# Decoder layer on one core: the opening written out by engine, and the output bias moved from TensorE to VectorE

## Chip, cores and metric

One core of one Trainium2 chip. The time is device microseconds of one execution; the number compared is the median of the timed runs.

## What is computed

For 16 sequences of 256 tokens and width 128 (x), and a context of 1601 rows of width 96 for each:

```python
x = x + attention(layernorm(x))             # one head of 128, with biases
x = x + cross(layernorm(x), context)        # 16 heads of 64, bias bo at the output
x = x + ffn(x)                              # router picks 31 tokens; small attention and MLP on them
# cross: q = x@Wq; k, v = context@Wk, context@Wv
#        sim = q k^T / 8; softmax over the 1601 rows; out@Wo + bo
```

All in float32 as far as the result goes. The cross attention is nearly all of the work: 16 sequences x 16 heads x 256 queries x 1601 keys.

## The kernel before, in words

The key and query weights of the cross attention are multiplied into one matrix per head (G, 96 x 128), the value and output weights into another (M). With these, scores are products of context rows and of the queries in the context's 96 columns, and the output is M applied to weighted sums of context rows. The arithmetic is float16 in two parts: a high part (AH, ChT, EH, Ch) and a low part (AL, ClT, EL, Cl).

**The stream.** A batch is 104 tiles: 8 pairs of heads, each with 13 tiles of 124 context rows. The stream runs over 16 x 104 tiles. For each tile n TensorE makes the scores ("st", L541 and L542, into PSUM banks 4 and 5), ScalarE takes exp into PF (L860), for each pair of tiles VectorE or ScalarE rounds PF to EH (L1042, L867), GpSimd takes the rest EL = PF - EH (L1512), and eight tiles later TensorE multiplies EH and EL with the context ("av", L558 and L560, into bank 6). After 13 tiles ScalarE copies the sums out (L876), GpSimd normalises them (L1520), TensorE transposes them ("turn_u", L615) and, for each four heads, multiplies with M ("proj", L605, bank 7) and VectorE adds the result to X (L1106). For the first quarter of heads the projection starts with products of a row of ones and the row xbo, the output bias bo (L603).

Beside it runs, for each batch, the preparation of the next: the shift of the softmax (an upper bound of the scores for each query) by "diff" and "base" products (L579, banks 2-3 and 0-1), a ReLU of ScalarE (L882), and "fold", a maximum of VectorE (L1065); then "placemax" transposes the maxima (L633), ScalarE scales them (L911) and a DMA of SyncE puts them into row 96 of AH (L1609). Further the layer norms, the self attention, the queries (L589, L896, L1074), the scale of the context, its split and its transposes (L626, L903), and the choice of tokens. The small steps share bank 7.

**Order.** The order is written by hand: plan(b, ...) gives each step of batch b a place, a tile number k, and whole_order(engine) lays the steps of all kinds into one list. Every engine runs through this list in the same order, save for steps that LATER moves by a few places for one engine. Engines skip steps in which they have nothing to do, and wait on semaphores for what others must have done, so a step stands behind whatever is ahead of it in its engine's list. SyncE follows TensorE's list. The steps ahead of the first tile form the opening; there, too, one list serves all engines. In it come in this order: layer norm and self attention of batch 0, the angles of the rotary embedding ("trig"), the scale of the context and of G ("sigma", "gtop"), G for the two halves of heads ("gm" q, parts 0 and 1, L708), its split ("gsplit", L958 and L1248), the context's split and transposes, the first queries, and the maximum of the first two heads. M (parts 2 and 3 of "gm", L720, copied by L1217) is made at places 0 to 3 of the stream. In the opening the small steps go round four banks, 7, 6, 0, 1.

BUSY names steps before which TensorE makes idle products of the identity (L520, results not used). keep_busy(step) issues them ahead of the step's own wait.

## Time and profile before

| | us |
|---|---|
| median of three timed runs (2243.27 to 2247.11) | 2245.14 |
| the profiled execution | 2249.61 |
| its span in the profile | 2248.4 |
| TensorE busy | 2154.0 |
| GpSimd busy | 1926.4 |
| ScalarE busy | 1831.9 |
| VectorE busy | 1781.7 |

All numbers below come from the one profiled execution, whose own time lies 1.2 us above its span and 4.5 us above the median of the timed runs. PE is TensorE, PEld its weight loads, DVE VectorE, ACT ScalarE, POOL GpSimd, SPq the DMA issues of SyncE. Matmuls overlap, and their ends are modelled: the distance between the starts of two, not their duration, says what one costs. In a group "xN" is the number of instructions; a float32 product counts two.

### The profile page before, as it was taken

How to read it: one execution, taken by the hardware profiler on the slowest of the kernel's cores; microseconds unless marked ns; L12 is line 12 of the kernel's file. 1: busy time of each engine (PE TensorE's matmuls, PEld its weight loads, DVE VectorE, ACT ScalarE, POOL GpSimd, SP SyncE). 2: the span in 40 equal slices, each digit the busy share in tenths (PEclk: the TensorE clock that was granted, in tenths of full speed). 3: DMA queues.
4: the chain of work that ended last, by engine and by line, in shares of the span. 5: the costliest groups of instructions: out<-in, count | busy, mean ns of one | idle time of the engine just before them, and what ended most of it. 6: DMA issues, size and time to landing. Idle time of an engine off the chain costs nothing.

```text
span 2248.4 us, 58064 instructions
## 1 busy us (share of the span) xinstructions
PE 2154.0 (96%) x22151; PEld 1574.0 (70%) x22151; DVE 1781.7 (79%) x3728; ACT 1831.9 (81%) x3125; POOL 1926.4 (86%) x1112
## 2 busy tenths in 40 slices
PE   7899999999999999999999999999999999999998
PEld 4677777777777767777777777767777777676665
DVE  6777888787887888878787788877868788886755
ACT  5888888888888888888788887888878888888862
POOL 2799999999998989898898898888978898898982
PEclk9999999999999999999999999999989999999999
DMA  3110000000000000000000000000000000000000
GB/s 69 37 43 13 2 9 5 2 13 2 13 2 4 11 2 13 2 13 2 11 13 2 13 2 2 13 2 13 2 11 12 2 13 2 2 1 2 2 8 13
DMA packets 17221, 22.15 MB, mean 10 GB/s; under 512 B 5601, under 2 KB 14834, under 8 KB 16946
## 3 DMA queue, kind: packets, MB, share of 16 engines
q1 hardware_dynamic: 15842, 18.24, 3.0%
q8 instruction: 178, 2.92, 0.5%
q14 instruction: 97, 0.79, 0.1%
q10 hardware_dynamic: 1104, 0.20, 0.1%
HBM read 16.20 MB, written 2.10 MB: 8 GB/s over the span
## 4 chain that ended last, share of the span: by engine, by line
PE 68%; DVE 12%; ACT 10%; issue 8%; POOL 3%; DVEq 0%; ACTq 0%; POOLq 0%
PE PS L541 12%; PE PS L579 12%; PE PS L542 11%; PE PS L558 10%; PE PS L560 9%; PE PS L605 4%; DVE EH L1042 4%; ACT PF L860 3%; DVE over L1065 3%; POOL EL L1512 2%; ACT EH L867 2%; ACT over L882 2%; PE PS L589 2%; PE PS L615 2%; DVE junk L1308 1%
## 5 line engine op out<-in xcount | busy, mean ns | idle before, releaser
L1512 POOL TENSOR_TENSOR EL<-PF,EH 124x1024 f16<-124x1024 f32 x828 | 1760.8, 2149 | 229.1 <-DVE EH L1042 111.2
L860 ACT ACTIVATE PF<-PS 124x512 f32<-124x512 f32 x1664 | 973.9, 603 | 251.5 <-PE PS L542 240.4
L558 PE MATMUL PS<-Ch,EH 123*128 123x97 f16 (+1 forms) x6656 | 769.8, 208 | 22.0 <-POOL EL L1512 11.2
L560 PE MATMUL PS<-Cl,EL 123*128 123x97 f16 (+1 forms) x6656 | 766.5, 208 | 0.0
L1042 DVE TENSOR_SCALAR_CACHE_REDUCE EH<-PF 124x1024 f16<-124x1024 f32 x621 | 745.1, 1209 | 9.2 <-ACT PF L860 9.0
L558 PEld LDWEIGHTS PS<-Ch,EH 123*128 123x128 f16 (+1 forms) x6656 | 611.4, 98 | 186.7 <-issue 61.1
L560 PEld LDWEIGHTS PS<-Cl,EL 123*128 123x128 f16 (+1 forms) x6656 | 600.8, 98 | 171.6 <-issue 4.6
L1065 DVE CUSTOM_DVE_ANT_1 over<-over,PS 128x806 f32<-128x806 f32 x512 | 506.0, 988 | 200.0 <-ACT over L882 110.8
L541 PE MATMUL PS<-AH,ChT 97*124 97x512 f16 x1664 | 649.6, 390 | 9.9 <-ACT PF L860 5.8
L542 PE MATMUL PS<-AL,ClT 96*124 96x512 f16 x1664 | 637.1, 383 | 0.0
L882 ACT ACTIVATE over<-PS 128x806 f32<-128x806 f32 x512 | 434.4, 848 | 36.1 <-PE PS L579 15.5
L541 PEld LDWEIGHTS PS<-AH,ChT 97*124 97x124 f16 x1664 | 226.7, 136 | 108.1 <-ACT PF L860 35.6
L579 PE MATMUL PS<-ChT,AH 96*128 96x403 f16 x1024 | 263.5, 338 | 13.7 <-DVE pmax L1065 13.5
L579 PE MATMUL PS<-KD,AH 96*128 96x403 f16 x1024 | 263.0, 338 | 0.8 <-ACT over L882 0.4
L542 PEld LDWEIGHTS PS<-AL,ClT 96*124 96x124 f16 x1664 | 228.3, 137 | 32.8 <-issue 0.6
L867 ACT ACTIVATE EH<-PF 124x1024 f16<-124x1024 f32 x211 | 223.7, 1061 | 0.0
L1074 DVE SCALAR_TENSOR_TENSOR AL<-PS,qscale,AH 96x512 f16<-96x512 f32 x128 | 95.5, 746 | 133.2 <-ACT AH L896 133.1
L1520 POOL TENSOR_TENSOR Un<-U,rden_u 128x384 f32<-128x384 f32 x127 | 114.6, 903 | 17.4 <-DVE rden_u L1095 17.4
L896 ACT ACTIVATE AH<-PS,qscale 96x512 f16<-96x512 f32 x128 | 87.5, 684 | 23.0 <-PE PS L589 22.9
L605 PE MATMUL PS<-M,UT 128*128 128x128 f32 x768 | 105.3, 283 | 0.1
L579 PEld LDWEIGHTS PS<-ChT,AH 96*128 96x128 f16 x1024 | 78.9, 99 | 34.7 <-DVE pmax L1065 19.2
L605 PEld LDWEIGHTS PS<-M,UT 128*128 128x128 f32 x768 | 91.9, 191 | 4.4 <-ACT UT L887 0.5
(234 smaller groups left out, 1816.2 us busy)
## 6 DMA issues: line engine op xcount, KB each, us to landing
Cf<-in_ctx SPq DMA_DIRECT2D x16, 546.0 KB
X<-in_x SPq DMA_DIRECT2D x16, 128.0 KB, 2.5
out_x<-X SPq DMA_DIRECT2D x16, 128.0 KB, 1.7
msk<-in_attention_mask SPq DMA_DIRECT2D x4, 256.0 KB, 4.3
AH<-mh SPq DMA_DIRECT2D x63, 2.0 KB
Cf<-in_ctx SPq DMA_DIRECT2D x16, 53.6 KB
xWqT<-in_xWqT SPq DMA_DIRECT2D x2, 256.0 KB, 7.5
xWo<-in_xWo SPq DMA_DIRECT2D x2, 256.0 KB, 4.2
```

The costliest lines, as they stand in the source:

```text
L541: pe.matmul(o, ChT[j][:, t, :], AH[:, cs], start=True, stop=False)
L542: pe.matmul(o, ClT[j][:, t, :], AL[:, cs], start=False, stop=True).then_inc(sg("st"), 1)
L558: pe.matmul(PS[:, 6, u0:u0 + DC + 1], EH[0:kr, r, qs], Ch[j][0:kr, t, :], start=(t == 0 and q == 0), stop=False, skip_group_check=True)
L560: m = pe.matmul(PS[:, 6, u0:u0 + DC + 1], EL[0:kr, r, qs], Cl[j][0:kr, t, :], start=False, stop=(t == KT - 1), skip_group_check=True)
L579: m = pe.matmul(PS[:, bank + n, 0:NKEY], AH[0:DC, ht * P:(ht + 1) * P], src[:, n * NKEY:(n + 1) * NKEY], start=True, stop=True)
L605: m = pe.matmul(PS[:, kb, t * D:(t + 1) * D], UT[:, t, c, :], M[:, qd * QC + c, :], start=(c == 0 and qd > 0), stop=(c == QC - 1))
L860: act.activation(PF[:, n % PRING, :], PS[0:KP, 4 + n % 2, :], ACT.Exp).then_inc(sg("ex"), 1)
L867: act.activation(EH[:, r - 1:r + 1, :], PF[:, f - 1:f + 1, :], ACT.Copy, scale=KEEP).then_inc(sg("eh_act"), 1)
L882: act.activation(over[:, i % 2, :, :], PS[:, 2:4, 0:NKEY], ACT.Relu).then_inc(sg("relu"), 1)
L1042: dve.tensor_scalar(EH[:, r - 1:r + 1, :], PF[:, f - 1:f + 1, :], KEEP, None, ALU.mult, ALU.add, accum_out=esum[:, r // 2:r // 2 + 1]).the ...
L1065: dve.tensor_tensor_reduce(out=o, in0=o, in1=PS[:, 0:2, 0:NKEY], scale=1.0, scalar=LEAST, op0=ALU.add, op1=ALU.max, accum_out=pmax[:, b % ...
L1512: pool.tensor_tensor(EL[:, r - 1:r + 1, :], PF[:, f - 1:f + 1, :], EH[:, r - 1:r + 1, :], ALU.subtract).then_inc(sg("lo_pool"), 1)
```

## The change

- The opening is written out for each engine on its own (a new function opening(engine)), instead of one list for all. The products of M move from places 0 to 3 of the stream into the opening, two of them into other banks (0 and 2 instead of 6), with waits of their own; the fifth diff and base wait for them. The split of the second half of G goes ahead of the first placing of the maxima, the fold of the first maxima ahead of the scale of the second half of G, the products of the probabilities' transposes ahead of that of G's maximum.
- Idle products: one more at sa_t and at sa_qk, one less at sa_o, none at sa_turn, ctx_t and placemax; new ones ahead of diff 1 and base 1 to 3.
- The output bias: xbo is loaded as a row for each of the 128 partitions, and a new step "bias" of VectorE adds it to X of the batch (128x256), two places after the step sa_f of that batch; for batch 0 at the end of the opening. The products of ones and xbo at the first projection of each batch go. The projection's add waits for it once.
- GpSimd no longer fills a row of ones, and fills the last row of ChT only after the angles are done (a wait on trig_in).
- SyncE loads the two bias columns b_q and b_k ahead of the weights w_q and w_k.
- All places of the stream stay as they are, but for the products of M.

```diff
--- before.py
+++ after.py
@@ -156,7 +156,6 @@
                  (SEL_PLACE - 2, ("sel_count", b - 1, 0)), (SEL_PLACE + 3, ("sel_count", b - 1, 1)),
                  (SEL_PLACE + 13, ("sel_rank", b - 1))]
     if b == 0:
-        todo += [(k, ("gm", q, part)) for k, (q, part) in enumerate(((0, 2), (0, 3), (1, 2), (1, 3)))]
         todo += [(9, ("ln_stats0", 1)), (12, ("ln0", 1))]
         todo += [(10 + 4 * x, ("load_x", x)) for x in range(2, B)] + [(72, ("load_rest",))]
         todo += [(10, ("ctx_max", 1)), (18, ("sigma", 1)), (22, ("ctx_scale", 1))]
@@ -167,12 +166,37 @@
     if n < B:
         todo += [(TILES + k, step) for k, step in ahead(n) if k < 0]
         split = AV_LAG + 17 * (b == 0)
-        todo += [(split + 0, ("ctx_hi", n, 0)), (split - 1, ("ctx_hi", n, 1))]
+        todo += [(split, ("ctx_hi", n, 0)), (split - 1, ("ctx_hi", n, 1))]
         todo += [(split + 4, ("ctx_lo", n, 0)), (split + 8, ("ctx_lo", n, 1))]
         todo += list(zip(TURN_PLACES, transposes_of(n))) + [(TURN_PLACES[1] + 1, ("keys", n))]
         q = [k + 9 * (b == 0) for k in SA_PLACES]
         todo += list(zip((*q[:6], q[5] + 5, q[5] + 10, q[6]), self_attention(n)[2:]))
+        todo += [(q[6] + 2, ("bias", n))]
     return sorted(todo + beside.get(b, []), key=lambda x: x[0])
+
+
+def opening(engine):
+
+    stats, norm, turn, qk, val, sc, probs, att, stats1, norm1, x2 = self_attention(0)
+    high, low = context_of(0)[:2], context_of(0)[2:]
+    turns = transposes_of(0)
+    folds = [maximum(0, ht) for ht in range(4)]
+    moved = [("gm", q, part) for q, part in ((0, 2), (0, 3), (1, 2), (1, 3))]
+    if engine == "pe":
+        out = [turn, qk, ("wvo",), sc, ("sigma", 0), ("gm", 0, 0), ("gm", 0, 1), val, probs, ("gtop", 0), att]
+        out += turns[:2] + [("gm", 1, 0), ("gm", 1, 1), ("load_ctx", 1), x2, ("q", 0, 0)] + folds[0] + folds[1] + [("gtop", 1)]
+        out += folds[2] + folds[3] + turns[2:3] + moved[:1]
+        return out + [("placemax", 0, 0, 2)] + moved[1:2] + turns[3:] + moved[2:3] + [("q", 0, 1)] + moved[3:]
+    if engine == "act":
+        out = [turn, ("trig",), qk, sc, probs] + high + [("gsplit", 0)] + turns[:2] + [x2, ("q", 0, 0)]
+        out += [f[0] for f in folds] + [("gsplit", 1)] + turns[2:3]
+        return out + [("placemax", 0, 0, 2)] + turns[3:] + [("q", 0, 1)]
+    if engine == "dve":
+        out = [stats, norm, ("trig",), qk, ("ctx_max", 0), ("wvo",), sc, ("sigma", 0), ("gmax", 0), ("ctx_scale", 0), val]
+        out += [("gtop", 0), att, stats1, ("gsplit", 0), norm1, ("keys", 0), x2] + low + [("q", 0, 0)]
+        out += folds[0] + [("gmax", 1)] + folds[1] + [("gtop", 1)] + folds[2] + folds[3]
+        return out + [("gsplit", 1)] + moved[:3] + [("q", 0, 1)] + moved[3:] + [("bias", 0)]
+    return [stats, ("consts",), ("more_consts",), stats1]
 
 
 def whole_order(engine):
@@ -183,16 +207,7 @@
     def put(n, kind, *a):
         stream.append((n + shift.get(kind, 0), len(stream), (kind, *a)))
 
-    first = self_attention(0)
-    turns = transposes_of(0)
-    out += [first[0], ("consts",), *first[1:3], ("trig",), first[3], ("wvo",), ("ctx_max", 0), first[5], first[4]]
-    out += [("gm", 0, 0), ("gm", 0, 1), ("gmax", 0), ("sigma", 0), ("gtop", 0)]
-    split = context_of(0)
-    out += [first[6], ("more_consts",), ("ctx_scale", 0), first[7], first[8]] + split[:2]
-    out += [("gsplit", 0), split[2]] + turns[:2] + [("gm", 1, 0), ("gm", 1, 1)]
-    out += [first[9], split[3], ("load_ctx", 1), first[10], ("keys", 0), ("gmax", 1), ("q", 0, 0)]
-    out += maximum(0, 0)[:2] + [("gtop", 1)] + maximum(0, 0)[2:] + maximum(0, 1) + maximum(0, 2) + maximum(0, 3) + turns[2:3]
-    out += [("placemax", 0, 0, 2)] + turns[3:] + [("gsplit", 1), ("q", 0, 1)]
+    out += opening(engine)
     groups, todo = beside_plan(), []
     for n in range(TOTAL + AV_LAG):
         b, k = n // TILES, n % TILES
@@ -288,8 +303,7 @@
         wkT = sb("wkT", [P, P])
         wvo = sb("wvo", [P, P])
         cols = sb("cols", [P, 3])
-        xbo = sb("xbo", [1, P])
-        ones = sb("ones", [1, P])
+        xbo = sb("xbo", [P, P])
         crow = sb("crow", [P, P])
         fwq = sb("fwq", [P, 2, P])
         fwv = sb("fwv", [P, P])
@@ -410,7 +424,7 @@
         out_dram = out.rearrange("b (p t) d -> p b t d", t=T)
         X4 = X[:, :, :].rearrange("p (b t) d -> p b t d", t=T)
         rows = [slice(32 * b4, 32 * b4 + 32) for b4 in range(4)]
-        GM_BANKS = ((2, 3, 6, 6), (4, 5, 6, 6))
+        GM_BANKS = ((2, 3, 6, 0), (4, 5, 2, 6))
         HEAD_BANKS = (7, 6, 0, 1)
         TAIL_BANKS = (0, 1, 2, 3, 4, 6, 7)
         LAST_TURN = ("turn_u", B - 1, QD - 1, 1)
@@ -420,12 +434,11 @@
 
         M_CHUNKS = [of for m in range(HP // 2)
                     for of in (((2 * m, 0),), ((2 * m, P), (2 * m + 1, -64)), ((2 * m + 1, 64),))]
-        CONST_IDENT, CONST_TURNS, CONST_ALL = 5, 13, 29
+        CONST_IDENT, CONST_TURNS, CONST_ALL = 5, 12, 28
         HALVES = (slice(0, 7), slice(7, KT))
 
-        BUSY = {("sa_t", 0): 8, ("sa_qk", 0): 1, ("sa_turn", 0): 3, ("sa_o", 0): 2,
-                ("ctx_t", 0, 0, 0, 7): 2, ("sa_f", 0): 4, ("q", 0, 0): 4, ("diff", 0, 0): 3,
-                ("placemax", 0, 0, 2): 5,
+        BUSY = {("sa_t", 0): 9, ("sa_qk", 0): 2, ("sa_o", 0): 1, ("sa_f", 0): 4, ("q", 0, 0): 4, ("diff", 0, 0): 3,
+                ("diff", 0, 1): 2, ("base", 0, 1): 2, ("base", 0, 2): 2, ("base", 0, 3): 3,
                 ("turn_u", B - 1, QD - 1, 0): 4, ("proj", B - 1, QD - 1): 1, ("sel_row", B - 1): 17,
                 ("last_gather", NG - 1): 5, ("c_turn", NG - 1): 8, ("c_qkm", NG - 1): 3, ("c_tqk", NG - 1): 5,
                 ("c_sc", NG - 1): 4, ("c_texp", NG - 1): 12, ("c_att", NG - 1): 2, ("c_tatt", NG - 1): 1,
@@ -433,7 +446,7 @@
                 ("c_scat", NG - 1, 0): 2}
 
 
-        BUSY_LATER = (("sa_f", 0), ("q", 0, 0), ("diff", 0, 0), ("placemax", 0, 0, 2))
+        BUSY_LATER = (("sa_f", 0), ("q", 0, 0), *((k, 0, ht) for k in ("diff", "base") for ht in range(4)))
 
 
         order = whole_order("pe")
@@ -574,6 +587,8 @@
                         w.wait_ge(sg("relu"), i - 1)
                     else:
                         w.wait_ge(sg("fold"), i - 1)
+                    if i == 5:
+                        w.wait_ge(sg("m_done"), 3 if k == "diff" else 2)
                     src = KD[j][:, :] if k == "diff" else ChT[j][0:DC, :, :].rearrange("p t k -> p (t k)")
                     for n in range(2):
                         m = pe.matmul(PS[:, bank + n, 0:NKEY], AH[0:DC, ht * P:(ht + 1) * P],
@@ -598,12 +613,9 @@
                     for t in range(T):
                         if t == T - 1:
                             w.wait_ge(sg("ut_last" if last else "ut"), 1 if last else T * i)
-                        if qd == 0:
-                            w.wait_ge(sg("in_xbo"), 16)
-                            pe.matmul(PS[:, kb, t * D:(t + 1) * D], ones[0:1, :], xbo[0:1, :], start=True, stop=False)
                         for c in range(QC):
                             m = pe.matmul(PS[:, kb, t * D:(t + 1) * D], UT[:, t, c, :], M[:, qd * QC + c, :],
-                                          start=(c == 0 and qd > 0), stop=(c == QC - 1))
+                                          start=(c == 0), stop=(c == QC - 1))
                     m.then_inc(sg("pj_mm"), 1)
                 elif k == "turn_u":
                     b, qd, t = s.a
@@ -712,8 +724,12 @@
                         w.wait_ge(sg("in_xm"), 96)
                         if (q, part) == (0, 2):
                             w.wait_ge(*last_of_head(6))
+                        elif (q, part) == (0, 3):
+                            w.wait_ge(sg("fold"), 4)
+                        elif (q, part) == (1, 2):
+                            w.wait_ge(sg("relu"), 4)
                         else:
-                            w.wait_ge(sg("m_done"), 2 * q + part - 2)
+                            w.wait_ge(sg("m_done"), 1)
                         for c in range(QC):
                             of = M_CHUNKS[(2 * q + part - 2) * QC + c]
                             for n, (j, first) in enumerate(of):
@@ -1102,6 +1118,7 @@
                 elif k == "proj":
                     b, qd = s.a
                     w.wait_ge(sg("pj_mm"), i)
+                    w.wait_ge(sg("bo_added"), b + 1)
                     w.wait_ge(sg("pj_x"), i - 1)
                     dve.tensor_tensor(X[:, T * b:T * b + T, :], PS[:, bank_of(s), 0:T * D].rearrange("p (t d) -> p t d", d=D),
                                       X[:, T * b:T * b + T, :], ALU.add).then_inc(sg("pj_x"), 1)
@@ -1203,6 +1220,13 @@
                     dve.scalar_tensor_tensor(out=X2T[:, 1, b % 2, :], in0=X2T[:, 0, b % 2, :], scalar=-KEEP / REST,
                                              in1=PS[:, bank_of(s), 0:S], op0=ALU.mult,
                                              op1=ALU.add).then_inc(sg("x2_lo"), 1)
+                elif k == "bias":
+                    b, = s.a
+                    w.wait_ge(sg("xn2"), i)
+                    w.wait_ge(sg("in_xbo"), 16)
+                    dve.tensor_tensor(X[:, T * b:T * b + T, :], X[:, T * b:T * b + T, :],
+                                      xbo[:, :].rearrange("p (o d) -> p o d", o=1).to_broadcast([P, T, D]),
+                                      ALU.add).then_inc(sg("bo_added"), 1)
                 elif k == "wvo":
                     w.wait_ge(sg("wvo_mm"), 1)
                     w.wait_ge(sg("in_wvo"), 64)
@@ -1465,7 +1489,7 @@
             for s in orders["pool"]:
                 k, i = s.kind, s.i
                 if k == "consts":
-                    const(pool.memset(ones[:, :], 1.0), pool.memset(lower[:, :, :, :], 1.0), pool.memset(headmask[:, :], 1.0),
+                    const(pool.memset(lower[:, :, :, :], 1.0), pool.memset(headmask[:, :], 1.0),
                           pool.memset(blockmask[:, :], 1.0))
                     for f in range(FD // 2):
                         inv = float(np.float32(1.0) / np.power(np.float32(ROPE_BASE), np.float32(2 * f / FD)))
@@ -1492,6 +1516,7 @@
                     for j in range(2):
                         const(pool.memset(Ch[j][:, :, DC:DC + 1], 1.0), pool.memset(Cl[j][:, :, DC:DC + 1], 1.0))
                     const_ready()
+                    w.wait_ge(sg("trig_in"), 1)
                     for j in range(2):
                         const(pool.memset(ChT[j][DC:DC + 1, :, :], SHIFT_ROW))
                     const_ready()
@@ -1560,17 +1585,17 @@
                              c[b, NC - (KT - KFULL):NC, :].rearrange("(o t) d -> o t d", o=1)).then_inc(sg("in_ctx"), 16)
 
             load_x(0)
+            for j, n in enumerate(("b_q", "b_k")):
+                sp.dma_start(cols[:, j:j + 1], a[n].rearrange("(p o) -> p o", o=1)).then_inc(sg("in_wqk"), 16)
             for n, t in (("w_qT", wqT), ("w_kT", wkT)):
                 sp.dma_start(t[:, :], a[n]).then_inc(sg("in_wqk"), 16)
-            for j, n in enumerate(("b_q", "b_k")):
-                sp.dma_start(cols[:, j:j + 1], a[n].rearrange("(p o) -> p o", o=1)).then_inc(sg("in_wqk"), 16)
             load_context(0)
             halves = [slice(4 * q, 4 * q + 4) for q in range(2)]
             for q in range(2):
                 for n, t in big.items():
                     sp.dma_start(t[:, halves[q], :],
                                  a[n].rearrange("(j p) n -> p j n", p=P)[:, halves[q], :]).then_inc(sg(f"in_xg{q}"), 16)
-            sp.dma_start(xbo[:, :], a["xbo"].rearrange("(o n) -> o n", o=1)).then_inc(sg("in_xbo"), 16)
+            sp.dma_start(xbo[:, :], row("xbo")).then_inc(sg("in_xbo"), 16)
             load_x(1)
             w.wait_ge(sg("wvd_zero"), 1)
             for js in halves:
```


## Rows read from the trace of the kernel before

**Rows 1.** Busy time by stage: window, length, then each engine, granted clock, DMA share, GB/s
```profile
49.90:55.70 5.80, 5.32 (x31) 2.93 (x30) 5.15 (x9) 5.71 (x11) 4.28 (x2) 1.00 0.01 1
...
100.00:1000.00 900.00, 873.34 (x9212) 645.86 (x9211) 735.39 (x1518) 769.68 (x1318) 817.09 (x456) 1.00 0.03 9
...
640.00:660.00 20.00, 19.15 (x225) 14.25 (x223) 15.70 (x31) 18.84 (x32) 18.32 (x11) 1.00 0.01 2
```

**Rows 2.** Chain that ended last, share of the span by engine
```profile
PE 68%; DVE 12%; ACT 10%; issue 8%; POOL 3%; DVEq 0%; ACTq 0%; POOLq 0%
```

**Rows 3.** Timeline of the opening, 28 to 42 us: start, us, engine, line, operation
```profile
28.73 0.99 DVE L1065 CUSTOM_DVE_ANT_1 over<-over,PS 128x806 f32<-128x806 f32 x1
...
30.45 0.99 DVE L1065 CUSTOM_DVE_ANT_1 over<-over,PS 128x806 f32<-128x806 f32 x1 [0.72 <-PE PS L579]
...
34.55 0.99 DVE L1065 CUSTOM_DVE_ANT_1 over<-over,PS 128x806 f32<-128x806 f32 x1 [1.05 <-PE PS L579]
...
34.93 2.34 PE L520 MATMUL PS<-identb 128*128 128x512 f16 x5
...
37.52 0.27 ACT L911 ACTIVATE mh<-PS 4x128 f16<-4x128 f32 x1 [1.46 <-PE PS L633]
...
37.93 0.50 PE L626 MATMUL PS<-identb,Cl 124*96 124x124 f16 x6 [0.45 <-ACT mh L911]
...
39.31 0.64 PE L589 MATMUL PS<-X2T,G 128*96 128x256 f16 x4 [0.88 <-ACT ClT L903]
...
39.76 1.14 DVE L1248 SCALAR_TENSOR_TENSOR G<-PS,gscale,G 128x384 f16<-128x384 f32 x2 [3.95 <-ACT G L958]
...
41.00 0.64 PE L541 MATMUL PS<-AH,ChT 97*124 97x512 f16 x1 [1.05 <-issue]
```

**Rows 4.** Timeline, 45 to 56 us: products of M and two score products
```profile
45.46 1.05 PE L720 MATMUL PS<-xWo,wvd 128*128 128x128 f32 x8
...
49.97 0.38 PE L541 MATMUL PS<-AH,ChT 97*124 97x512 f16 x1
...
55.67 0.38 PE L541 MATMUL PS<-AH,ChT 97*124 97x512 f16 x1
```

**Rows 5.** Chain in order of time: first and last of 32 pieces of L603
```profile
116.72 0.41 PE PS L603 x2
...
2137.23 0.41 PE PS L603 x2
```

**Rows 6.** Adds of VectorE by source line: duration min/median/max ns, first and last start
```profile
L1106 DVE TENSOR_TENSOR X<-PS,X x64: 408/418/426, 119.6 to 2210.1; 128x256 f32<-128x256 f32 x64
...
L1379 DVE TENSOR_TENSOR KX<-fqkT,headmask x12: 676/679/2505, 815.1 to 1912.5; 128x512 f32<-128x512 f32 x12
```

**Rows 7.** GpSimd's main operation: its group on the page, and one at 814.92
```profile
L1512 POOL TENSOR_TENSOR EL<-PF,EH 124x1024 f16<-124x1024 f32 x828 | 1760.8, 2149 | 229.1 <-DVE EH L1042 111.2
...
814.92 2.13 POOL L1512 TENSOR_TENSOR EL<-PF,EH 124x1024 f16<-124x1024 f32 x1 [0.64 <-issue]
```

**Rows 8.** Timeline, 8 to 14 us
```profile
8.58 2.86 POOL L1496 MEMSET ChT<- 1x1612 f16 x2
...
8.60 1.46 DVE L1274 TENSOR_SCALAR turns<-trig 128x32 f32<-128x32 f32 x1
...
11.70 0.46 ACT L934 ACTIVATE kT<-PS,cols 128x256 f32<-128x256 f32 x1
...
11.97 1.45 DVE L1116 TENSOR_REDUCE cmx<-Cf 124x1 f32<-124x1248 f32 x1 [0.47 <-DMA Cf<-in_ctx]
```

**Rows 9.** Timeline, 15 to 20 us, VectorE
```profile
15.41 0.96 DVE L1224 TENSOR_REDUCE gmx<-PS 128x1 f32<-128x768 f32 x1 [1.01 <-PE PS L708]
...
19.71 0.61 DVE L1192 SCALAR_TENSOR_TENSOR X<-PS,rden,X 128x128 f32<-128x128 f32 x2 [0.60 <-PE PS L686]
```

**Rows 10.** Busy time and granted clock in 2 us of the opening
```profile
32.00:34.00 2.00, 1.47 (x6) 0.41 (x4) 1.00 (x2) 0.84 (x1) 0.00 (x0) 0.50 0.00 0
```

**Rows 11.** DMA issues: a row of 64 KB spread over the partitions, us to landing
```profile
ln1r<-in_ln SPq DMA_DIRECT2D x1, 64.0 KB, 3.4
```

## The prediction

> **What bounds the kernel now.** I read three things in this order: the windows of busy time by stage, the chain that ended last, and the timeline of the first 60 us.
>
> In the long middle all engines are filled, TensorE most: from 100 to 1000 us it is busy 873 of 900 us, at a granted clock of 1.00, GpSimd 817, ScalarE 770, VectorE 735 [rows 1]. The chain puts 68% of the span on TensorE, 12% on VectorE, 10% on ScalarE and 3% on GpSimd [rows 2]. So the middle is limited by TensorE with short stretches in which another engine holds it up; a microsecond of TensorE work taken out there is worth most of a microsecond, and one added on VectorE little, unless it comes where VectorE or GpSimd is late.
>
> The opening is different: it is one chain of short steps through all engines, and TensorE stands idle or works on idle products. The first score product of the stream starts at 41.00 and the tenth at 55.67 [rows 3, 4].
>
> **The bias, in the stream.** It leaves TensorE: per batch two products of one row, each two instructions. The chain holds 32 such pieces (two for each of 16 batches), each of 0.41 us, the first at 116.72, the last at 2137.23 [rows 5]. All of them lie on the chain, so 32 x 0.41 = 13.1 us go if nothing takes their place. They are not hidden by the weight loads of their neighbours, since each piece moves the next one's start.
>
> In their place come 16 adds of VectorE over 128x256 f32. The nearest row is the add of the projection, with the same shape but one input in PSUM: 0.418 us [rows 6]. The new add has both inputs in SBUF. For that kind the trace has KX: four times a batch group 128x512 in 0.68 us, but 2.5 us at the longest [rows 6], and that one starts at 815.10 while GpSimd works on EL from 814.92 for 2.13 us [rows 6, 7]: it ends when that is over, plus its own 0.68 us. So the new add costs 0.42 us when GpSimd is between operations, and up to 0.42 + 2.13 = 2.55 us when it comes just behind the start of one. GpSimd is busy 817 of 900 us [rows 1], so most adds meet one, on the mean halfway: 0.91 x 1.07 + 0.42 = 1.4 us, or 22 us of VectorE in all. The trace does not show what GpSimd loses by it; nothing to 0.42 us each, up to 7 us in all.
>
> The Trainium skill, "SBUF — State Buffer", section "Who interferes with whom", says the same against this change: an operation of VectorE with two SBUF inputs and an operation of GpSimd that reads SBUF lock each other out for a whole instruction. By it every add is exposed; the KX row agrees for the waiting side.
>
> Behind the add wait, on VectorE, the roundings of EH and the folds of the maximum of that place (58 of 104 in a batch), and behind the rounding GpSimd and the products with EL. What covers it: from 640 to 660, around that place, VectorE is busy 15.7 of 20 us, GpSimd 18.3 and ScalarE 18.8 [rows 1]. VectorE has 4.3 us of room for 1.4 us, but in pieces, and GpSimd has 1.7. I take 0.3 us per batch on the end time, 5 us in all (bounds: 0, when it falls into a gap, and 13, when nothing of TensorE's gain is kept). Net: 13 - 5 = **8 us less** (between 13 and nothing). The new wait of the projection on the add has long been met: the projection of the batch comes a whole batch later.
>
> **The opening.** Step by step, with times of the profiled run.
>
> Constants: the trigonometry of VectorE runs into GpSimd's fill of ChT (8.58 for 2.86 us); one small tensor_scalar takes 1.46 us, until the first half of the fill is over [rows 8], a second one waits for the second half, and the key copy of ScalarE starts at 11.70 [rows 8]. With the fill held until the trigonometry is done, the copy can start about 1.5 us earlier (my estimate: nearly all of that 1.46, and some of the second). But in the new order of VectorE the maximum of the context stands ahead of the score maximum, and its data arrive at 11.97; it runs until 13.42 [rows 8]. This gain is eaten there: 0.
>
> Self attention of batch 0: the transposes of the probabilities stand in TensorE's list behind the maximum of G (15.41 for 0.96) [rows 9] and three idle products; after the change they are issued before them. What comes next is VectorE, which has sigma, G and context in front of the value add. I take 0.6 us at the X update (19.71 now) [rows 9] and, because normalising no longer stands behind a context split, 1.1 us at the second transposed input.
>
> Maximum of the first two heads: the first fold starts at 28.73 and the last at 34.55 [rows 3]. The scaling of the second half of G stands ahead of the first fold now and goes between the folds; and from 30 us the clock granted falls, 0.50 at 32 to 34 [rows 10], while the loop waits on folds. With idle products inside the loop it should stay up. A step took 1.72 us while the clock was full (28.73 to 30.45) and 2.05 after it, (34.55 - 30.45)/2 [rows 3]. I take 2.0 us off the end of the last fold: 33.5 instead of 35.5.
>
> From there to the first score product: now five idle products (34.93 for 2.34 us) stand before the transposed maximum, ScalarE places it at 37.52, and the first score product goes at 41.00, right behind the low part of G on VectorE (39.76 for 1.14) [rows 3]. After the change the low part of G is done by about 35, and the placing by 34.5, which with the same 3.5 us until the data are in place gives 38.0. But TensorE's own list is longer: four groups of products for M at 1.05 us each [rows 4], two groups of context transposes at 0.5 and the queries at 0.64 [rows 3], 0.3 for the placing, all after about 32.5: 6.1 us, 38.6. So the first score product starts at **38.6 instead of 41.0**.
>
> First ten tiles: now 14.7 us (41.00 to 55.67), of which the first five go at the pace of M (one group and its copy for each), the next five take 5.7 us, 1.14 each [rows 3, 4], ScalarE busy nearly throughout: 5.71 of 5.80 us [rows 1]. Without M among them all go at that pace: nine spacings, 10.3 to 11 us. Gain 3.8.
>
> Sum of the opening: 2.4 + 3.8 = 6.2, I say **6 us less** (4 to 9: 4 if the clock falls during the M products, as they would then take twice as long). Nothing after it is tied to absolute time, so the shift should last. The bias row now loads as 128 rows; 64 KB rows of this kind land in 3.4 us [rows 11]. It stands ahead of the loads for M, which are wanted only after 32 us: hidden. One fill less on GpSimd: hidden.
>
> **The sum.** 8 + 6 = 14 us. Span 2248.4, profiled run 2249.6; that gives 2235.6 for this one, and against the median of the three timed runs (2245.14) **2231**. A measurement of this kernel can tell about 0.2% (4.5 us) from no change.
>
> **Rivals.**
> - *VectorE and GpSimd take the bias back.* The adds stand in the stretch where GpSimd has under 2 us of room in 20; each late rounding makes GpSimd late and TensorE waits for EL as long as it gained. For it: GpSimd already waits 111 us in all for roundings of VectorE [rows 7], so roundings come late often. Against: at that place the chain runs on TensorE and ScalarE. It gives the opening alone, 6 us: 2239. Chance 0.16.
> - *The opening is bound elsewhere.* The M products fall into a low clock or the placing of the maximum arrives late; opening 1 to 2 us, bias 8: 2235.5. Chance 0.09.
> - *The add costs more than the products (slower).* One mechanism: each add waits a whole GpSimd operation, 2.55 us, holds GpSimd's next for 0.42 us, and the delay reaches TensorE. Slower than before by over 0.2% needs (4.5 + 6 + 13.1)/16 = 1.5 us per batch to come through. If all of 2.55 does: 16 x 2.55 - 13.1 - 6 = 22, 2267; if 1.7: 2253. Chance 0.04.
> - *No net effect at all*, when the adds take back the products' time and the early start is used up waiting in the first batch, where ScalarE and VectorE are the slower ones: 0 to 2 us, 2244. Chance 0.05.
> - My forecast, 7 to 22 us less, 2223 to 2238: 0.66.
>
> Range 2223 to 2240: below, the two upper bounds together (13 + 9 = 22); above, the first two rivals. Faster by over 0.2% (below 2240.6): 0.87; within: 0.08; slower: 0.05.
>
> **What would show it.** Per batch in the stream: 0.8 us less between the same score products. First score product near 38.6 and the tenth near 49.5; clock 1.00 from 28 to 40. The new add in rows of 0.42 us at the least and over 2 us at the most. The forecast is wrong if the spacing of batches is unchanged (first rival), if the tenth score product still comes after 53 (second), or if waits of TensorE for EL or of GpSimd for roundings grow by more than 13 us (third).

## The result, and the profile of the changed kernel

The changed kernel takes 2219.35 us (median of 4 runs, 2214.64 to 2221.95); the kernel before took 2244.2 in the 4 runs beside it. The ratio is 0.9888, 95% interval 0.9863 to 0.9913: 25 us less where I had forecast 14, and below the range I gave (2223 to 2240). The sign and both mechanisms held; the size of the bias part did not.

The profiled run took 2221.95 us, span 2220.7 (before 2249.6 and 2248.4). Busy time in the long middle, to be held against [rows 1]; columns as there:

```profile
100.00:1000.00 900.00, 874.28 (x9264) 647.49 (x9263) 743.67 (x1535) 776.14 (x1331) 821.95 (x460) 1.00 0.03 10
```

TensorE is as full as it was. It does more in the same 900 us: 9264 matmuls instead of 9212. The stage view therefore shows the gain only as more work for the same time, not as less busy time. The chain by engine [rows 2] reads almost as before:

```profile
PE 68%; DVE 12%; ACT 10%; issue 7%; POOL 2%; DMA 0%; SPq 0%; DVEq 0%; ACTq 0%; POOLq 0%
```

**Where the time went** comes from a comparison of the starts of the same score product in both profiles. There are 1664 of them, 104 per batch. "Before minus after" is 3.0 us at the first, 6.8 at the tenth, and 6.8 still at the 51st. Between the 51st and the 54th product of *each* of the 16 batches it grows by 1.15 us, and between the 54th and the 63rd it shrinks by 0.02 to 0.05 (0.2 in the first and the last batch). Nothing else changes it until 940 us; a batch without other work has a period of 128.5 us instead of 129.7. At the end it is 27.6. So: opening 6.8, bias 17.5 (1.12 in most batches), together about 24.3; the other 3 us of this pair of profiles come in steps of 1 to 6 us, of both signs, in batches 6 to 15 (counted from 0), where the granted clock of one or the other kernel falls (below).

**The opening.** Timeline of the changed kernel to the first score product; start, us, engine, line, operation, and in brackets the idle time before it:

```profile
8.52 0.18 DVE L1298 TENSOR_SCALAR turns<-trig 128x32 f32<-128x32 f32 x1
...
9.35 2.82 POOL L1521 MEMSET ChT<- 1x1612 f16 x2 [0.91 <-DVE trig L1304]
9.72 0.47 ACT L950 ACTIVATE kT<-PS,cols 128x256 f32<-128x256 f32 x1 [0.20 <-DVE qT L1188]
11.01 1.45 DVE L1133 TENSOR_REDUCE cmx<-Cf 124x1 f32<-124x1248 f32 x1 [1.39 <-DMA Cf<-in_ctx]
...
19.47 0.61 DVE L1209 SCALAR_TENSOR_TENSOR X<-PS,rden,X 128x128 f32<-128x128 f32 x2 [1.43 <-PE PS L698]
...
27.48 0.99 DVE L1081 CUSTOM_DVE_ANT_1 over<-over,PS 128x806 f32<-128x806 f32 x1 [0.80 <-ACT over L898]
...
32.89 0.99 DVE L1081 CUSTOM_DVE_ANT_1 over<-over,PS 128x806 f32<-128x806 f32 x1 [0.72 <-PE PS L594]
...
37.99 0.38 PE L554 MATMUL PS<-AH,ChT 97*124 97x512 f16 x1
...
48.91 0.38 PE L554 MATMUL PS<-AH,ChT 97*124 97x512 f16 x1
```

The small operation of the trigonometry takes 0.18 us instead of 1.46, and the key copy starts 2.0 us earlier (9.72 against 11.70) [rows 8]. Of that, 0.24 us are left at the X update of the self attention (19.47 against 19.71) [rows 9]. The first fold starts 1.25 us earlier, the last 1.66 (32.89 against 34.55) [rows 3], the first score product 3.0 and the tenth 6.8 [rows 3, 4]. In between lies a stretch, 14 to 21 us, in which the granted clock falls:

```profile
14.00:21.00 7.00, 6.95 (x37) 5.94 (x37) 4.88 (x21) 4.08 (x10) 0.00 (x0) 0.51 0.73 139
21.00:40.00 19.00, 17.44 (x117) 10.78 (x116) 14.70 (x36) 10.01 (x17) 0.92 (x2) 1.00 0.12 34
```

The granted clock is at its lower level (1.2 GHz) from 14.0 us for 6.8 us, and TensorE is busy 6.95 of 7.00 us with 37 products. From 21 to 40 us, where the kernel before had its fall (0.50 at 32 to 34) [rows 10], it is 1.00. What the fall between 14 and 21 us took, two profiles without it show (in the part on the prediction).

**The bias.** The timeline around the first projection, of the kernel before:

```profile
115.77 0.38 PE L541 MATMUL PS<-AH,ChT 97*124 97x512 f16 x1
115.99 0.38 PE L542 MATMUL PS<-AL,ClT 96*124 96x512 f16 x1
116.65 0.48 PE L603 MATMUL PS<-xbo,ones 1*128 1x128 f32 x2
117.06 0.94 PE L605 MATMUL PS<-M,UT 128*128 128x128 f32 x6
117.93 0.48 PE L603 MATMUL PS<-xbo,ones 1*128 1x128 f32 x2
118.34 0.94 PE L605 MATMUL PS<-M,UT 128*128 128x128 f32 x6
119.11 0.38 PE L541 MATMUL PS<-AH,ChT 97*124 97x512 f16 x1
```

and of the changed one:

```profile
108.98 0.38 PE L554 MATMUL PS<-AH,ChT 97*124 97x512 f16 x1
...
109.77 1.57 PE L617 MATMUL PS<-M,UT 128*128 128x128 f32 x12
111.17 0.38 PE L554 MATMUL PS<-AH,ChT 97*124 97x512 f16 x1
```

From score product to score product it is 119.11 - 115.77 = 3.34 us before and 111.17 - 108.98 = 2.19 after: 1.15 us for what I had priced at 2 x 0.41. The chain says why. Before, it has 0.41 for two instructions of L603 and then **0.86** for six of L605, twice, in all 2.54; the changed kernel has one piece for twelve:

```profile
109.93 1.41 PE PS L617 x12
```

0.70 for six, not 0.86. A one-row product (two instructions) costs 0.41 and slows the six instructions behind it by 0.16.

**The add** by source line (duration in ns at the least, median and most):

```profile
L1227 DVE TENSOR_TENSOR X<-X,xbo x16: 410/1266/1550, 39.1 to 1983.3; 128x256 f32<-128x256 f32 x16
```

The mean is 1.13 us (18.0 us for 16), where I had estimated 1.4. The 16 do not scatter: thirteen take 1.26 to 1.55 us and three 0.41 to 0.47. In nearly every batch the add meets GpSimd's operation at the same point.

### The profile page after: what moved, and what is told of

Its sections match the earlier page's. It is cut to its first block, busy times and chain, and to the rows that moved or that the text cites. A ratio compares the mean times of both kernels' runs of the same rounds, so it can differ in the third digit from the quotient of the medians.

```text
span 2220.7 us, 57952 instructions
## 1 busy us (share of the span) xinstructions
PE 2128.6 (96%) x22087; PEld 1559.0 (70%) x22087; DVE 1789.6 (81%) x3744; ACT 1830.5 (82%) x3125; POOL 1924.7 (87%) x1111
## 4 chain that ended last, share of the span: by engine, by line
PE 68%; DVE 12%; ACT 10%; issue 7%; POOL 2%; DMA 0%; SPq 0%; DVEq 0%; ACTq 0%; POOLq 0%
PE PS L554 12%; PE PS L594 12%; PE PS L555 11%; PE PS L571 10%; PE PS L573 9%; PE PS L617 4%; DVE EH L1058 4%; DVE over L1081 3%; ACT PF L876 3%; ACT over L898 2%; ACT EH L883 2%; POOL EL L1537 2%; PE PS L604 2%; PE PS L627 2%; DVE junk L1332 1%
## 5 line engine op out<-in xcount | busy, mean ns | idle before, releaser
L1537 POOL TENSOR_TENSOR EL<-PF,EH 124x1024 f16<-124x1024 f32 x828 | 1759.5, 2147 | 205.2 <-DVE EH L1058 110.3
L617 PE MATMUL PS<-M,UT 128*128 128x128 f32 x768 | 100.5, 281 | 0.1
```

The costliest lines, as they stand in the source:

```text
L617: m = pe.matmul(PS[:, kb, t * D:(t + 1) * D], UT[:, t, c, :], M[:, qd * QC + c, :], start=(c == 0), stop=(c == QC - 1))
L1537: pool.tensor_tensor(EL[:, r - 1:r + 1, :], PF[:, f - 1:f + 1, :], EH[:, r - 1:r + 1, :], ALU.subtract).then_inc(sg("lo_pool"), 1)
```

## The experiments

Ratios are to the kernel before, timed beside each version on the same chip. Its medians in the three groups of runs were 2245.23, 2244.95 and 2245.35 us.

**1. The bias alone.** The kernel before with the bias hunks of the change and its own opening:

```diff
-                        if qd == 0:
-                            w.wait_ge(sg("in_xbo"), 16)
-                            pe.matmul(PS[:, kb, t * D:(t + 1) * D], ones[0:1, :], xbo[0:1, :], start=True, stop=False)
...
+        todo += [(q[6] + 2, ("bias", n))]
```

> The kernel before with only the bias moved to the add of VectorE (opening as before). Theory now held (a bias product costs TensorE 1.15 us per batch and the add next to nothing): 16 x 1.1 = 18 us less than before, and the distance of two score products around the first projection of a batch shorter by 1.15 us. Rival (the price was right at 0.82 us per batch and the rest of the surplus came from the opening or from the granted clock): 13 us less or fewer. The first score product stays at 41.0 us, the tenth at 55.7.

2227.59 us (6 runs), 0.9920 [0.9903, 0.9937]: 17.6 us less. The same score products lie 1.12 us closer in each batch (1.15 at the projection), as in the changed kernel. The opening did not stay where I had it: the first score product comes at 42.57 us and the tenth at 57.25, not at 41.0 and 55.7, though no step of TensorE ahead of them was moved. In the five profiles with the old opening the tenth comes between 55.67 and 58.50 us, in the seven with the new one (experiments 8 and 9 left out) between 46.41 and 49.36. The pair compared above has the earliest of the five, so 6.8 us is at the low end of what such pairs show; the middle ones, 56.55 and 48.80, are 7.7 us apart.

**2. The opening alone.** The changed kernel with the one-row products back and no add:

```diff
-        todo += [(q[6] + 2, ("bias", n))]
...
+                        if qd == 0:
+                            w.wait_ge(sg("in_xbo"), 16)
+                            pe.matmul(PS[:, kb, t * D:(t + 1) * D], ones[0:1, :], xbo[0:1, :], start=True, stop=False)
```

> The changed kernel with the bias back on TensorE. Theory: the opening alone gives 6.8 us at the tenth score product, and 6 to 8 us in the end, with no further difference per batch. Rival (the early start brings a lasting gain in the stream): over 10 us.

2233.7 us (11 runs), 0.9948 [0.9929, 0.9966]: 11.5 us less. The tenth score product is 6.9 us earlier than before, the distance is 7.0 afterwards and stays there until the clock falls of the two kernels differ; the projections are as in the kernel before. So the opening is worth 7 us by this pair of traces. The medians of the two halves add up to 29 us, more than the 25 of the whole; the mean clock of the runs is 0.9938 here against 0.9903 before, and experiment 11 says what that is worth.

**3. No bias at all** (the output bias bo is left out of the result):

```diff
-                            pe.matmul(PS[:, kb, t * D:(t + 1) * D], ones[0:1, :], xbo[0:1, :], start=True, stop=False)
```

> The kernel before without any bias (bo is left out of the output), neither product nor add. The difference to the run with the bias on VectorE is the price of 16 adds. Theory: the adds are hidden, price under 2 us in all (0.04 us per batch); 18 us less than before. Rival, the prediction's own step: 0.3 us per batch, 5 us in all, so this one 5 us faster than the run with the adds.

2228.06 us (6 runs), 0.9922 [0.9905, 0.9939], and between the same score products the same as experiment 1, down to the 0.03 us taken back. The add of VectorE costs nothing that reaches TensorE.

**4. The bias product with all 128 rows.** Each row of `ones` holds 1/128 and `xbo` is spread over 128 rows, so the sum is the same:

```diff
-                            pe.matmul(PS[:, kb, t * D:(t + 1) * D], ones[0:1, :], xbo[0:1, :], start=True, stop=False)
+                            pe.matmul(PS[:, kb, t * D:(t + 1) * D], ones[:, :], xbo[:, :], start=True, stop=False)
```

> The kernel before with the bias product made of 128 rows (a full matrix of 1/128 times a row repeated 128 times) instead of one row. If the one-row form is what makes a bias product and its neighbours dear, a projection with bias costs four more instructions at the plain pace of 0.118 us: 0.47 us per batch over none instead of 1.13, and the time falls by some 10 us. If any product there costs as much, no change.

2237.97 us (10 runs), 0.9967 [0.9954, 0.9980]: 7 us less by the medians, where I had expected some 10; between score products it is 0.70 us per batch, 11 in all. Chain of this kernel at the first projection:

```profile
117.51 0.29 PE PS L603 x2
117.80 0.67 PE PS L605 x6
118.47 0.22 PE PS L603 x2
118.69 0.67 PE PS L605 x6
```

Against two times 0.41 and 0.86: the sum is 1.85 instead of 2.54. The instructions are as many and the columns as many; 0.69 of the 1.13 us lie in the one-row form, 0.44 in the two products themselves. The six behind a full product take 0.67.

**5. The one-row product last in its group** instead of first:

```diff
-                            pe.matmul(PS[:, kb, t * D:(t + 1) * D], ones[0:1, :], xbo[0:1, :], start=True, stop=False)
...
+                            m = pe.matmul(PS[:, kb, t * D:(t + 1) * D], ones[0:1, :], xbo[0:1, :], start=False, stop=True)
```

> The kernel before with the one-row bias product last in its group instead of first. If the one-row form makes the instructions after it slow, the price per batch changes; if it is the change of form itself, in and out, it stays: the same 1.15 us per batch over no bias, so no difference of place 53 against the kernel before.

2252.94 us in a single run, mean clock 0.987. Chain at the first projection:

```profile
119.45 0.73 PE PS L602 x6
120.19 0.41 PE PS L606 x2
120.60 0.86 PE PS L602 x6
121.47 0.41 PE PS L606 x2
121.88 0.36 PE PS L541
```

The sum of the four pieces of the projection is 2.41, but what follows the last one-row product is now a score product, and its piece is 0.36 instead of the 0.22 that the other score products near it have. Between score products the projection costs what it did in the kernel before (difference 0.00). The first six, with no one-row product ahead of them, take 0.73, the next six, behind one, 0.86: it is the work behind that is slowed, whatever it is. Why, the runs leave open. Moving the product does not help.

**6. Three dependent operations in place of the add** (add, subtract, add), each waiting for the one before:

```diff
+                    for x in range(3):
+                        m = dve.tensor_tensor(X[:, T * b:T * b + T, :], X[:, T * b:T * b + T, :],
+                                              xbo[:, :].rearrange("p (o d) -> p o d", o=1).to_broadcast([P, T, D]),
+                                              (ALU.add, ALU.subtract, ALU.add)[x])
+                        m.then_inc(*((sg("bo_added"), 1) if x == 2 else own_step()))
+                        if x < 2:
+                            w.wait_ge(*own_steps())
```

> The changed kernel with three operations of VectorE in place of the one add (add, subtract, add of the same row, each waiting for the one before), at the same place. Theory (the add lies in time that VectorE has to spare at that place, so that up to some 3 us per batch are covered): under 1 us more in all. Rival (the add is just covered, at the limit): 0.5 us or more per batch, 8 us in all.

2255.03 us (10 runs), 1.0037 [1.0021, 1.0053]: slower than the kernel before, and 36 us above the changed kernel. I had expected under 1 us more, with 8 us as the rival; both were far too low.

**7. Two dependent adds** (the bias is added twice, so the result holds 2 bo); the edit is that of experiment 6 with two adds:

```diff
+                    for x in range(2):
...
+                                              ALU.add)
```

> The changed kernel with two adds of the bias row in place of one (the output has bo twice). One add costs 0.03 us per batch of end time, three cost 2.1. Theory (the place covers a fixed time of VectorE, about 1.9 us with the first add's wait, and what is beyond comes through in full; two adds take about 2.6 us): 0.7 us per batch, 11 us. Rival (a second add makes VectorE miss a whole operation of GpSimd at the key difference): 2 us per batch at once.

2241.93 us in a single run, mean clock 0.993 as in the changed kernel's runs, so 23 to 24 us more for the second add. In a batch without chosen-token work the second add costs 1.67 us between the same score products, the second and third operation of experiment 6 together 2.09. The timeline around the add in batch 2, with one add:

```profile
379.21 1.27 DVE L1227 TENSOR_TENSOR X<-X,xbo 128x256 f32<-128x256 f32 x1
380.40 0.98 DVE L1081 CUSTOM_DVE_ANT_1 over<-over,PS 128x806 f32<-128x806 f32 x1
...
382.45 0.57 DVE L1074 TENSOR_TENSOR KD<-ChT 96x806 f16<-96x806 f16 x1
382.66 2.35 POOL L1537 TENSOR_TENSOR EL<-PF,EH 124x1024 f16<-124x1024 f32 x1 [0.18 <-issue]
```

with two:

```profile
381.16 3.54 DVE L1228 TENSOR_TENSOR X<-X,xbo 128x256 f32<-128x256 f32 x2
384.62 0.98 DVE L1081 CUSTOM_DVE_ANT_1 over<-over,PS 128x806 f32<-128x806 f32 x1
...
386.67 0.57 DVE L1074 TENSOR_TENSOR KD<-ChT 96x806 f16<-96x806 f16 x1
386.88 2.35 POOL L1541 TENSOR_TENSOR EL<-PF,EH 124x1024 f16<-124x1024 f32 x1 [2.47 <-issue]
```

and with three, the fold's wait on TensorE as well:

```profile
382.81 4.00 DVE L1228 TENSOR_TENSOR X<-X,xbo 128x256 f32<-128x256 f32 x3
...
387.79 0.52 PE L594 MATMUL PS<-ChT,AH 96*128 96x403 f16 x2 [1.50 <-DVE pmax L1081]
...
389.00 2.35 POOL L1541 TENSOR_TENSOR EL<-PF,EH 124x1024 f16<-124x1024 f32 x1 [2.92 <-issue]
```

One add takes 1.27 us and GpSimd is idle for 0.18 before its next operation; two take 3.54 us, more than twice one, and GpSimd stands idle for 2.47. Singly, the first add takes 1.27 us in all three kernels, the second 2.24, the third 0.43: the second ends just behind the end of a further whole operation of GpSimd. That operation's successor then has to wait for the rounding EH, which stands behind the adds on VectorE; the fold behind them is late as well, and TensorE waits for it. What is covered is the same in both experiments: 3.54 - 1.67 = 1.87 us with two adds, 4.00 - 2.09 = 1.91 with three. So this place hides about 1.9 us of VectorE, the whole of one add and 0.6 us more, and what is beyond comes through in full. I had thought of the cover as some 3 us wide, and that fell with experiment 6. The 1.9 us that I then named for experiment 7 held; what I had wrong there was the length of two adds, 2.6 us against the measured 3.54, and so 0.7 us per batch against 1.67.

Why one add is free, the kernel before shows at the same place of a batch:

```profile
651.14 1.13 DVE L1058 TENSOR_TENSOR KD<-ChT 96x806 f16<-96x806 f16 x1 [0.39 <-ACT ChT L903]
...
652.58 0.99 DVE L1065 CUSTOM_DVE_ANT_1 over<-over,PS 128x806 f32<-128x806 f32 x1 [0.22 <-PE PS L579]
```

There the key difference KD takes 1.13 us with 0.39 us of idle time ahead of it and 0.22 behind; after the change 0.57 with neither. From its start to that of the next operation the add takes 1.19 us (380.40 - 379.21). The 0.56 that KD no longer takes and the 0.61 of idle time are 1.17 of them. KD, too, has both inputs in SBUF, and its 0.56 us are of the kind that the add now has; I read them as a wait for GpSimd that was there already and has moved from one operation to another. No experiment tests this reading by itself; that one add is free is shown by experiment 3.

**8. No idle products inside the maximum's loop:**

```diff
-                ("diff", 0, 1): 2, ("base", 0, 1): 2, ("base", 0, 2): 2, ("base", 0, 3): 3,
```

> The changed kernel without the nine idle products of the loop over the first maxima (before diff 1 and base 1 to 3). Theory (they hold the clock there): the clock falls to 0.5 for 3 to 7 us between 28 and 40 us, the first score product comes 1 to 4 us later than at 38.0. Rival (they hold nothing, the shorter loop is due to the order alone): no difference.

2220.34 us (4 runs), 0.9882 [0.9852, 0.9912]. The first score product starts at 39.58. Both falls of the clock are in this run: 0.61 from 14 to 21 us, and from 29 to 37:

```profile
29.00:37.00 8.00, 7.14 (x36) 5.04 (x37) 5.67 (x18) 3.78 (x6) 0.00 (x0) 0.57 0.00 1
```

Kernels with the changed opening, of which only the first fall is in the profile, started it at 37.88 to 38.44 (four of them). So the products in the loop keep the clock up (none of the eight profiles with them has a fall there) and are worth 1.1 to 1.7 us, too little for the times of whole runs to show.

**9. GpSimd's fill of ChT not held back** for the trigonometry:

```diff
-                    w.wait_ge(sg("trig_in"), 1)
```

> The changed kernel without GpSimd's wait for the angles ahead of its fill of ChT. Theory (the prediction's step: the angles are held up by the fill, but what is gained is eaten by the wait for the context's data): key copy of ScalarE some 1.5 us later (11.2 instead of 9.7), the X update of self attention (19.47) within 0.5 us. Rival: the X update and the first score product come a microsecond or more later.

2217.61 us in a single run. The small operation takes 1.46 us again and the key copy starts at 11.62 instead of 9.72, yet the first score product comes at 38.77, 0.3 to 0.9 us behind those four. The X update of the self attention comes at 20.68, against 19.47 to 20.36 in the four; I had expected it within 0.5 us of 19.47. The wait costs nothing that shows and, by these single profiles, brings under 1 us at the first score product, not the 1.9 that the key copy gains.

**10. Idle products in TensorE's gaps of the stream.** The changed kernel, with products that write a free bank of PSUM ahead of two waits of the chosen tokens' work (a), and ahead of a third (b):

```diff
+                    if s.a[0] < NG - 1:
+                        fill(kb, 10)
                     w.wait_ge(sg("c_hn2"), i)
...
+                    if b4 == 0 and gq < NG - 1:
+                        fill(bank_free(s), 4 if gq < 2 else 12)
                     w.wait_ge(sg("c_proc"), gq + 1)
...
+                        if s.a in after_scores:
+                            w.wait_ge(sg("c_sc0"), after_scores[s.a] + 1)
+                            fill(7, 6)
                         w.wait_ge(sg("fold"), i - 1)
```

> The changed kernel with idle products in three waits of the stream in each of the first three groups of chosen tokens: ten ahead of the transposes that wait for the second normalised input, four (twelve in the third group) ahead of the first scatter. In the trace of the changed kernel the granted clock fell at 942.5, 1352, 1482, 2021 and 2147, each time within 4 us of such a wait, for 30.7 us in all. Theory (what differs from run to run is this clock, 1.6 us for each 0.001 of its mean): the falls at 942, 1482, 2021 and 2147 go, the mean clock comes to 0.996 or more and the time falls by 5 to 8 us against the changed kernel, with less spread. Rival (the idle products delay the stream as much as they save): no gain, the spacing of batches 6, 10 and 14 grows.

> The kernel with idle products in the stream's waits, with six more ahead of the base products that wait for a fold behind the score maximum of the chosen tokens (the gap of 1.9 us at place 91 of batches 5, 9 and 13, where the clock fell at 1349 in the last run). Theory: no fall of the clock in the stream at all; 1 to 2 us faster than with the three other fills, 2211, and 8 us faster than the changed kernel. Rival: the falls are gone but the six products delay, no gain over 2212.8.

(a) 2212.77 us (5 runs), 0.9850 [0.9827, 0.9873]; (b), which has all three, 2208.93 us (5 runs), 0.9838 [0.9815, 0.9861]. The first place in the changed kernel, from the timeline of TensorE:

```profile
939.46 0.51 PE L594 MATMUL PS<-KD,AH 96*128 96x403 f16 x2
942.72 0.69 PE L829 MATMUL PS<-ident,GTt 128*128 128x128 f32 x2 [2.74 <-DVE hn L1370]
...
943.41 0.63 PE L554 MATMUL PS<-AH,ChT 97*124 97x512 f16 x1
```

and in version (b):

```profile
937.27 0.51 PE L608 MATMUL PS<-KD,AH 96*128 96x403 f16 x2
937.62 2.32 PE L537 MATMUL PS<-identb 128*128 128x512 f16 x10
940.53 0.44 PE L845 MATMUL PS<-ident,GTt 128*128 128x128 f32 x2 [0.59 <-DVE hn L1388]
...
940.91 0.38 PE L565 MATMUL PS<-AH,ChT 97*124 97x512 f16 x1
```

In the first, TensorE stands for 2.74 us and the score products behind it take 0.63 us instead of 0.38: the clock has gone to its lower level at 942.5, within the pause. In the second the pause is filled up to 0.59 us, the wait itself ends no earlier (3.26 us from the fold's product to the transposes in both), and the next products run at 0.38.

**11. The changed kernel once more**, timed beside (b):

> The changed kernel itself once more, beside the next one, on the same chip. 2219 us as before; its mean clock between 0.990 and 0.996, and its time 1.6 us for each 0.001 of it.

2217.7 us (5 runs, 2215.97 to 2224.0), 0.9871 [0.9850, 0.9892]. Version (b) lies 8.8 us under it, and all five of its runs (2207.94 to 2214.45) under all five of these. It beats both kernels, by 36 us the one before. Not all of the 8.8 us need be the idle products': in the pair of profiles, 10.6 us apart, 3.0 are there at the first score product (38.44 against 35.49), where the two kernels do not differ, since (b) happens to have no fall in its opening; the other 7.6 come between the first and the last score product. Version (a) has 6.7 there.

A straight line through the times of all 115 timed runs of this study, with one level for each kernel and one slope for all, gives 1.60 us (95% interval 1.42 to 1.78) for each 0.001 of the run's mean granted clock, with a scatter of 1.8 us about it. Worked out for a clock of 1.000, the kernel before would take 2230.7, the changed one 2208.4 and 2207.5 in its two sets of runs, versions (a) and (b) 2207.5 and 2207.8: within this scatter the idle products change the clock and nothing else. The bias alone is then 15.9 us less than before (17.5 by the score products), the opening alone 6.4, together 22.3, and the changed kernel is 22.3 to 23.2 less. The two halves add up; what they seemed to have over was clock.

## Why the prediction was wrong in size

**The step that failed** is the one under "The bias, in the stream": "so 32 x 0.41 = 13.1 us go". It counted the pieces of the bias product itself and took the twelve products around them as unchanged. Each one-row product also slows the products behind it by 0.16 us: 1.15 us per batch and not 0.82, 18.4 us in all and not 13.1. The rows were there: the chain has 0.86 for six products behind a one-row one, and 1.41 for twelve where a projection has no bias [rows 5 show only the pieces of L603]. Reading the piece that goes and not its neighbours was the mistake; experiments 1, 3, 4 and 5 show it.

**The second term of that part** was too high, by nearly as much: the 0.3 us per batch taken for the add, 5 us in all, were 0.03 in most batches, 0.9 us in all, and none of it the add's (experiment 3 has it too). The price of the operation was right in kind and near in size: 0.41 us at the least, 1.27 at the median and 1.55 at the most, against bounds of 0.42 and 2.55 and a mean of 1.4. That the mean came near is partly luck: it was worked out for adds that meet GpSimd at any point, and they meet it at the same one, 1.27 us long, in most batches. What the Trainium skill says in "SBUF — State Buffer", section "Who interferes with whom", of VectorE operations with two SBUF inputs, that they contend with a GpSimd operation that reads SBUF, is borne out by the median of 1.27 us where the same addition with one input in PSUM takes 0.42 [rows 6]. What I had wrong is what an exposed operation costs the end time: here 1.9 us of VectorE are covered, and the add needs 1.27. Together the two terms gave 8 us where the runs show 16 to 18; of the 9.5 us between 8 and 17.5, 5.3 are the first term's and 4.1 the second's.

**The opening** came out as forecast, in part by luck: 6.8 us at the tenth score product against 6.2 by the sum and 6 as taken. Its steps, one by one: the end of the last fold 33.9 (33.5 forecast), the first score product 37.99 (38.6), the tenth 48.91 (about 49.5), clock 1.00 from 28 to 40. The gain in the first ten tiles, 3.8 us, was right in size: they take 10.92 us, 14.67 before (for 3.4 of which, from 41.0, the clock was at its lower level, which the reasoning left out). But the time of the first score product rests on two errors that cancel. I had not foreseen a fall of the clock between 14 and 21 us. Version (b) of experiment 10, whose opening is the same, has in this stretch

```profile
14.00:21.00 7.00, 6.33 (x55) 4.85 (x55) 6.53 (x24) 4.50 (x9) 0.93 (x2) 1.00 0.71 134
```

55 products instead of 37, at 1.00 instead of 0.51. It and the kernel of experiment 6, the two profiles without a fall there, have the X update at 17.39 and 17.21 us, the end of the last fold at 31.4 and 31.2, the first score product at 35.49 and 35.30 and the tenth at 46.41 and 46.62: 9.3 and 9.1 us earlier than in the kernel before, just above what I gave for the opening (4 to 9). So the steps ahead of the first fold gain more than I had taken: it starts at 24.97 and 24.77, 3.8 to 4.0 us earlier, where I had 0.6 to 1.1. The 1.5 us of the trigonometry I had called eaten by the wait for the context's data; but that wait was itself 1 us shorter or more (the maximum of the context starts at 11.01, 10.61 and 10.42 in the three profiles, 11.97 before). In the profiled run, with the low clock, 0.24 us were left at the X update where I had taken 0.6. How much of the 2.3 to 2.5 us at the X update is the trigonometry's and how much the new order's, no run separates. Whether the clock falls between 8 and 21 us changes from profile to profile, with either opening, and no run tells what decides it.

**The rivals.** "VectorE and GpSimd take the bias back" (2239) fell: GpSimd's waits for roundings are 110.3 us, 111.2 before [rows 7]. It is not far off, though: a second add brings it about (2241.93 us in its one run). "The opening is bound elsewhere" fell with the tenth product at 48.91, "no net effect" with experiments 1 and 2. "The add costs more than the products" needed 1.5 us per batch to come through; one add lets through nothing, and three operations instead of one, with 2.1, make that case (2255).

**The clock of the stream** stood nowhere in the sum. In the kernel before it is worth about 14 us (2245 against 2230.7 at full clock), and it scatters by some us from run to run. A change that moves the stream against its own pauses draws anew there: the mean clock of the changed kernel's runs is 0.9935 and of the kernel before 0.9903, 5 us by the slope of the line. Whether these 0.003 belong to the change or to the draw, the runs leave open; the sets of runs scatter by as much (0.9917 with the bias alone, 0.9938 with the opening alone).

## What to carry to other kernels

Price an instruction that is to go by the distance of its neighbours with and without it, not by its own piece of the chain: a product over one row of the array cost 0.41 us and 0.16 more in the products behind it. An operation that waits for another engine can be free where the place has time to hide it, or where it takes over a wait that a later operation would have had; test by doubling it how far that goes: here the place hid 1.9 us, one add of 1.27 but not two. And where TensorE is the bound, look at its pauses of 1 to 4 us: filling them with idle products shortened no wait and gave 8 to 9 us through the clock. When a forecast of an opening comes out, look at a second profile: here profiles with one fall of the clock fewer had the first score product 2.5 us earlier.

## What the runs showed of the hardware that I had not expected

- **The one-row product.** Two instructions with one row of weights took 0.41 us on the chain, with 128 rows 0.22 to 0.29, at the same number of columns; behind them six products took 0.86, 0.67 behind the 128-row form and 0.70 in a projection without bias.
- **The clock falls in a stream that is 96% busy.** The granted clock of the kernel before is at its lower level eight times, for 3.4 to 13.7 us each; that of the changed one seven times; in version (b) it is 1.00 over the whole span. The eleven falls in the streams of the first two begin 2.1 to 4.0 us after TensorE began a pause of 0.86 to 3.99 us, but not each such pause has one behind it. Batch 11 (counted from 0) takes 140.5 us in the kernel before, with a fall of 13.7, and 133.1 in the changed one, of which the bias explains 1.1. The longest fall of the kernel before begins at 1635.0 us, behind one of the shortest of these pauses:

```profile
1632.57 0.71 PE L834 MATMUL PS<-XA,KX 32*128 32x128 f32 x4 [0.86 <-DVE XA L1422]
```

```profile
1635.00:1651.00 16.00, 16.00 (x101) 10.67 (x100) 7.36 (x15) 7.82 (x13) 7.47 (x6) 0.57 0.06 18
```

  In the changed kernel the same stretch of time, some 19 us further on in the stream, has 161 products instead of 101, at a clock of 1.00. It has the same pause of 0.86 us too, at 1612.5, and no fall behind it.

```profile
1635.00:1651.00 16.00, 15.86 (x161) 11.70 (x159) 13.64 (x25) 13.73 (x25) 14.70 (x9) 1.00 0.00 1
```

  TensorE is busy by the profile for all of the first: a full row of busy time can be work at half the speed, and only the count and the clock beside it tell.
- **Two dependent adds cost more than two adds.** With a wait between them the second ends behind a whole further operation of GpSimd: 3.54 us for two against 1.27 for one, and GpSimd idle for 2.47 after them. The third, right behind, takes 0.43.
